# A graph network on one core: the counts of destinations are gathered from a table in DRAM

## What is computed

```python
def _sage_conv(x, src, dst, Wp, bp, Wl, bl, Wr):
    h = relu(x @ Wp.T + bp)
    agg = segment_sum(h[src], dst, num_segments=N)
    cnt = segment_sum(ones(src.shape[0]), dst, num_segments=N)
    agg = agg / maximum(cnt, 1.0)[:, None]
    return agg @ Wl.T + bl + x @ Wr.T
```

## Time and profile before

| | |
|---|---|
| median of 3 runs | 1517.86 us (1517.79 to 1518.0) |
| profiled execution | 1517.14 us, of which the span from first to last instruction is 1515.0 us |
| TensorE busy | 1492.6 us, 99% |
| VectorE busy | 981.2 us, 65% |
| ScalarE busy | 687.1 us, 45% |
| GpSimd busy | 578.6 us, 38% |
| DMA engines | 193 GB/s in the mean |

### The profile page before, as it was taken

The page is one execution under the profiler, slowest core; times in us unless marked ns, Lnnn a source line. Parts: engine busy times, 40 slices in busy tenths (PEclk is TensorE's granted clock), DMA queues, the critical chain, the costliest instruction groups (busy, mean ns, idle before and its releaser), DMA issues.

```text
span 1515.0 us, 21400 instructions
## 1 busy us (share of the span) xinstructions
PE 1492.6 (99%) x7295; PEld 1221.5 (81%) x7295; DVE 981.2 (65%) x2164; ACT 687.1 (45%) x1267; POOL 578.6 (38%) x534
## 2 busy tenths in 40 slices
PE   7999999999999999999999999999999999999997
PEld 5787887888888888888888888888888888888886
DVE  7999975655555687777565655557766666555552
ACT  5545452232233577767322323357676652322322
POOL 4737754344323100100434442323354366444323
PEclk9999999999999999999999999999999999999999
DMA  8897877555554878887645555489999986455434
GB/s 301 319 377 249 271 249 238 111 90 89 93 85 56 242 263 306 271 275 253 216 108 90 88 93 88 54 244 320 345 329 324 328 292 207 80 89 90 73 45 60
DMA packets 152855, 291.72 MB, mean 193 GB/s; under 512 B 19885, under 2 KB 19948, under 8 KB 152620
## 3 DMA queue, kind: packets, MB, share of 16 engines
q1 hardware_dynamic: 123708, 224.81, 43.3%
q0 software_dynamic: 28464, 64.51, 24.7%
q10 hardware_dynamic: 576, 1.05, 0.2%
HBM read 132.33 MB, written 157.92 MB: 192 GB/s over the span
## 4 chain that ended last, share of the span: by engine, by line
PE 89%; DMA 4%; DVE 3%; issue 2%; POOL 1%; ACT 1%; SPq 0%; POOLq 0%; ACTq 0%; DVEq 0%
PE bank L737 12%; PE bank L736 12%; PE bank L738 12%; PE bank L724 9%; PE bank L820 7%; PE bank L822 7%; PE bank L821 7%; PE bank L841 7%; PE bank L843 7%; PE bank L842 7%; DMA node_x<-xn 2%; DVE stats L1073 1%; DVE rows_out L1103 1%; DVE h_low L1047 1%; DMA rows_in<-node_x,sorted_src 1%
## 5 line engine op out<-in xcount | busy, mean ns | idle before, releaser
L736 PE MATMUL bank<-w_high,h_low 128*128 128x512 f32 x900 | 374.6, 416 | 0.0
L737 PE MATMUL bank<-w_low,h_high 128*128 128x512 f32 x900 | 356.3, 396 | 0.0
L738 PE MATMUL bank<-w_high,h_high 128*128 128x512 f32 x900 | 354.5, 394 | 0.0
L981 ACT ACTIVATE h_high<-h_pre 128x500 fp32r<-128x500 f32 x120 | 74.6, 622 | 449.0 <-DVE h_pre L1284 449.0
L594 POOL DMA_INDIRECT rows_in<-node_x,sorted_src x120 | 124.1, 1034 | 274.6 <-PE bank L724 199.8
L927 ACT ACTIVATE h_high<-bank 128x512 fp32r<-128x512 f32 x221 | 131.4, 595 | 155.2 <-PE bank L724 155.0
L738 PEld LDWEIGHTS bank<-w_high,h_high 128*128 128x128 f32 x900 | 169.3, 188 | 40.3
L1050 DVE TENSOR_TENSOR h_low<-bank,h_high 128x512 fp32r<-128x512 f32 x152 | 105.0, 692 | 146.4 <-ACT h_high L927 144.5
L961 ACT ACTIVATE xn<-rows_in,off,rstd 128x512 f32<-128x512 f32 x237 | 189.4, 806 | 13.6 <-issue 9.0
L820 PE MATMUL bank<-xt_low,w_high 128*128 128x500 f32 x480 | 194.5, 405 | 0.0
L736 PEld LDWEIGHTS bank<-w_high,h_low 128*128 128x128 f32 x900 | 169.8, 189 | 30.3
(11 more groups left out here) (127 smaller groups left out, 2209.1 us busy)
## 6 DMA issues: line engine op xcount, KB each, us to landing
node_x<-xn SPq DMA_DIRECT2D x237, 256.0 KB, 3.9
rows_in<-node_z SPq DMA_DIRECT2D x158, 256.0 KB, 4.4
node_z<-rows_out SPq DMA_DIRECT2D x142, 256.0 KB, 2.8
out<-rows_out SPq DMA_DIRECT2D x79, 256.0 KB, 3.5
rows_in<-x SPq DMA_DIRECT2D x78, 256.0 KB, 4.6
residual<-x SPq DMA_DIRECT2D x78, 256.0 KB, 4.3
node_z<-bias_z SPq DMA_DIRECT2D x16, 256.0 KB, 3.6
rows_in<-node_x SPq DMA_DIRECT2D x16, 256.0 KB, 2.6
```

The costliest lines, as they stand in the source:

```text
L736: nc.tensor.matmul(psum, low[:, k, :], w_high("r", l)[:, k, :], start=(k == 0), stop=False)
L737: nc.tensor.matmul(psum, high[:, k, :], w_low("r", l)[:, k, :], start=False, stop=False)
L738: last = nc.tensor.matmul(psum, high[:, k, :], w_high("r", l)[:, k, :], start=False, stop=(k == K - 1))
```

## The change

The counts no longer travel with the edges. The table of 128 x 128 counts is stored to DRAM as it is (by SP, one step after DVE's copy). When the edges are in order, GpSimd gathers the count of each edge's destination from this table, with an indirect DMA of 125 single numbers for each edge tile, 40 in all. They stand in GpSimd's program behind the load of `carry` and ahead of the row gathers. DVE takes the reciprocal in the first layer's edge phase, after the first step of it. The differences, their splitting, the masks, the look-up products and the reads of them go, and the stores of edges no longer wait for them. The work on the sorted edges is moved from step 61 to step 54.

```diff
-STEP_LOOKUP = 27
-LOOKUPS = 2
-STEP_SORTED = 61
+STEP_SORTED = 54
...
+        count_table = nc.dram_tensor("count_table", [P * P, 1], F32).ap()
...
+                    if l == 0 and i == STEP_COUNTED + 1:
+                        sp.wait_ge(counts_copied, 1)
+                        sp.dma_start(count_table.rearrange("(p c) a -> p (c a)", c=P), counts
+                                     ).then_inc(counts_stored, DMA)
...
-            def reach_mask(t):
...
             def store_edges(t):
 
                 pool.wait_ge(rows_placed, t // SPREAD + 1)
-                pool.wait_ge(count_read, t + 1)
...
+            def gather_counts(t):
+
+                G.indirect_dma_start(
+                    out=count_of[0:EDGE_ROWS, t:t + 1], out_offset=None, in_=count_table,
+                    in_offset=bass.IndirectOffsetOnAxis(ap=count_row[0:EDGE_ROWS, t:t + 1], axis=0)
+                ).then_inc(counts_gathered, DMA)
...
             for t in range(EDGE_TILES):
                 count_masks(t)
-            stored = 0
             for t in range(EDGE_TILES):
-                reach_mask(t)
-                if t % LOOKUPS == LOOKUPS - 1 and t >= 2 * LOOKUPS:
-                    store_edges(stored)
-                    stored += 1
-            for t in range(stored, EDGE_TILES):
                 store_edges(t)
...
+            pool.wait_ge(count_rows, 1)
+            pool.wait_ge(counts_stored, DMA)
+            for t in range(EDGE_TILES):
+                gather_counts(t)
...
-            def steps_of_counts():
...
-            def lookup(t):
...
-            def make_steps():
...
-            def count_digits():
...
-                V.reciprocal(share[0:EDGE_ROWS, :], in_order[0:EDGE_ROWS, :, 2]).then_inc(share_done, 1)
+                V.tensor_scalar(count_row[0:EDGE_ROWS, :], number[0:EDGE_ROWS, :], -1.0, None, ALU.add
+                                ).then_inc(count_rows, 1)
...
-            def read_count(t):
...
+            def shares():
+                dve.wait_ge(counts_gathered, DMA * EDGE_TILES)
+                V.reciprocal(share[0:EDGE_ROWS, :], count_of[0:EDGE_ROWS, :]).then_inc(share_done, 1)
...
+                    if l == 0 and s == 0:
+                        shares()
```

More of the change, by code:

```diff
@@ L15 @@
 DMA = 16
-CONSTS = 6
+CONSTS = 5
 IN_RING = 8
@@ L24 @@
 HOT_RING = 4
-STEP_RING = 4
 ROW_CHUNKS = 5
@@ L182, in sage_kernel @@
         edge_columns = residual[0:GROUPS, 1, 0:GROUP_ROWS]
-        counts, count_steps, steps_lo_f, steps_i0, steps_i1, steps_b = spare[0:6]
-        steps_i = [steps_i0.bitcast(I32), steps_i1.bitcast(I32)]
-        steps_b = steps_b.bitcast(BF16).rearrange("p (a c) -> p a c", a=2)
+        counts = spare[0]
         xt_high = [sb(f"xt_high{i}", [P, K * GROUP_ROWS], F32R) for i in range(2)]
@@ L223, in sage_kernel @@
         counts_copied = sem("counts_copied")
[L224 to L229, removed]
+        counts_stored = sem("counts_stored")
+        count_rows = sem("count_rows")
+        counts_gathered = sem("counts_gathered")
         share_done = sem("share_done")
@@ L766, in count @@
                                  start=(t == 0), stop=(t == EDGE_TILES - 1)).then_inc(counted, 1)
-            def steps_of_counts():
[L769 to L772, removed]
             def turn_carry():
                 pe.wait_ge(continues_done, 1)
-                pe.wait_ge(count_read, EDGE_TILES)
+                pe.wait_ge(counts_copied, 1)
                 nc.tensor.transpose(bank[2][0:EDGE_TILES, 0:EDGE_ROWS], continues[0:EDGE_ROWS, :],
                                     ident[0:EDGE_ROWS, 0:EDGE_ROWS]).then_inc(carry_turned, 1)
-            def lookup(t):
[L781 to L791, removed]
             def shift_p(l):
@@ L859, in _ @@
                             count((i - STEP_COUNT) * COUNTS + q)
-                    if l == 0 and i == STEP_COUNTED + 1:
-                        steps_of_counts()
                     if l == 0 and i == STEP_SORTED + 1:
                         turn_carry()
-                    if l == 0 and STEP_LOOKUP <= i < STEP_LOOKUP + EDGE_TILES // LOOKUPS:
-                        for q in range(LOOKUPS):
-                            lookup((i - STEP_LOOKUP) * LOOKUPS + q)
                     if l and i == STEP_SHIFT_P:
@@ L1214, in copy_carry @@
                 V.tensor_copy(carry_row[0:EDGE_TILES, :], bank[2][0:EDGE_TILES, 0:EDGE_ROWS]).then_inc(carry_copied, 1)
-            def read_count(t):
-                step, q = t // LOOKUPS, t % LOOKUPS
-                dve.wait_ge(looked_up, (step + 1) * LOOKUPS)
-                if step:
-                    dve.wait_ge(count_read, step * LOOKUPS)
-                V.scalar_tensor_tensor(out=unread[0:EDGE_ROWS, q, :], in0=column_no[0:EDGE_ROWS, 0:P],
-                                       scalar=lo_f[0:EDGE_ROWS, t:t + 1],
-                                       in1=bank[2 + step % 2][0:EDGE_ROWS, q * P:(q + 1) * P],
-                                       op0=ALU.is_equal, op1=ALU.mult, accum_out=edges[0:EDGE_ROWS, t, 2:3]
-                                       ).then_inc(count_read, 1)
+            def shares():
+                dve.wait_ge(counts_gathered, DMA * EDGE_TILES)
+                V.reciprocal(share[0:EDGE_ROWS, :], count_of[0:EDGE_ROWS, :]).then_inc(share_done, 1)
             def shift_part(l, m, k):
@@ L1326, in _ @@
                         copy_counts()
-                    if l == 0 and i == STEP_COUNTED + 2:
-                        count_digits()
                     if l == 0 and i == STEP_SORTED:
@@ L1332, in _ @@
                         copy_carry()
-                    if l == 0 and STEP_LOOKUP <= i - 1 < STEP_LOOKUP + EDGE_TILES // LOOKUPS:
-                        for q in range(LOOKUPS):
-                            read_count((i - 1 - STEP_LOOKUP) * LOOKUPS + q)
                     if 0 <= i - STEP_SPLIT_P < K:
```

32 lines of the change are left out of this document (2 added, 30 removed).

## The result

The changed kernel takes 1549.71 us in the median (1547.95 to 1551.35), the kernel before in the same rounds 1517.93 us. The ratio is 1.021, with an interval of 1.020 to 1.022. The forecast was 1537.9 us with a range up to 1547 us. So the sign was right, and the size was out of the range by 2.7 us: +31.8 us where +20.0 us stood.

A forecast was written before the change was run, and what follows sets the result against it. TensorE, busy 99%, bounds the kernel, but GpSimd's first row gathers decide when the edge phase starts. Row gathers 18.0 us later plus 2.0 us restart give +20.0 us: 1517.9 to 1537.9 us, range 1529 to 1547 us.

The forecast's parts named there:

- What goes: TensorE, node steps 27 to 46: look-up matmuls and the steps-of-counts product go, 6.8 us together; DVE and GpSimd savings costed at nothing.
- What moves: Sorted edges' work on DVE from 224.50 to 195.1 us, carries' store to 201.6, GpSimd free at 205.6.
- The restart: TensorE after its long wait at the first edge tile: slow transposes and first product, costing 2.0 us.
- The place: First layer's edge phase starts when GpSimd's first row gathers land, not when TensorE is free; one wait of 14 to 27 us.
- The rivals 3 and 4: 3: sorted edges late at DVE's step 54, 1541 us, chance 0.08; 4: low pitch, no slow restart, 1530 us, chance 0.15.
- Forty of them are 56 us: GpSimd, ahead of the row gathers: forty count gathers at 1.40 us pitch start the first row gather 18.0 us later.
- rival 2: GpSimd's queue fills and stalls 3.3 us among the count gathers, at the high pitch: +26.9 us, 1545 us; chance 0.15.
- I see nothing later that takes it back: TensorE from 249 us on has next to no idle time, so the delay stays to the end.
- Rival 1: Count gathers on GpSimd hidden before the row gathers, only savings stay: 1511 us at best; chance 0.05 faster, 0.02 within 0.2%.

## Why the forecast was too low

**Right.** *What goes*: TensorE's last node product starts at 240.08, as "at about 240 us" had it, and the steps 27 to 46 take 3.23 to 3.24 us each (the 3.42 us that the prediction names for a step of before is read a little low, transposes to transposes none takes under 3.44; nothing hangs on it). *What moves*: the order loads are issued at 185.96 (forecast 186) and DVE starts on the sorted edges, without a wait, at

```profile
195.21 0.18 DVE L1134 CAST sorted_src<-in_order 128x40 int32<-128x40 f32 x1
```

(forecast 195.1); the carries' store is at 202.23 (201.6). The stall ahead of the last store came again, 5.28 us this time, and fitted, because the stores as a whole ran early. *The restart*: 2.04 us, of a forecast of 2.0, and the two runs with products in the wait show that it is the idle time's. That the size is met so well is in part luck: the forecast was 1.7 us for the product and 0.4 us for the transposes, and it was 2.04 us for the product, while the slow transposes (0.76 instead of 0.41 us) were hidden, since the second tile followed the first more closely than before. *The place*: one wait, at the first edge tile, made by GpSimd's order. The Trainium skill says in "TensorE: Matmul & The Clock Gate", Part 1 (The HAM clock gate), that an idle array drops to 1.2 GHz; the trace agrees here, with a granted clock of 0.50 beside the 4.91 us. The 1.00 of the earlier trace rows beside a product as slow is no measurement: the trace of the kernel before has its first entry of the clock at 14.5 us, and there its matmuls go from 0.63 us (the one at 13.96) to 0.39 us (14.68). *The rivals 3 and 4* did not come: the sorted edges were in time, and the restart was slow.

**The step that failed: "Forty of them are 56 us ... The first row gather then starts at 205.6 + 56 = 261.6 us".** It started at 269.97, 8.4 us later. Three terms of it were off:
- The pitch is (268.47 + 1.50 - 207.43 - 2.19) / 40 = 1.51 us, not 1.40: 4.4 us. I stood between two rows and took a value between them. The issue takes as long as that of the stores in the earlier trace rows, 1,202 ns against 1,189 ns, though direction and size differ; the trait that the two share is the 125 rows. The run with 128 rows shows that it was this trait: 955 ns, in the same direction and with as many bytes for each row. So of these three it is the number of rows and neither the direction nor the bytes that made the difference, and I weighed three traits alike. No number but 125 and 128 was tried.
- The stall of rival 2 came, once: 268.47 - 264.78 = 3.69 us where the pitch is 1.50, 2.2 us. It stands ahead of the fortieth transfer: in the stores of edges in all 16 traces, among them the kernel before, where the first twenty stores stood among masks and not in a row; and in the counts in all five traces with forty 125-row gathers ahead of the row gathers. It didn't come with twenty gathers, with forty of 128 rows or with forty spread among the row gathers. "It has been seen once, under a loaded DMA" was my reason for 0.15, and it was a poor one: what had been seen once in one try came every time. That a queue fills, as rival 2 supposes, no run shows.
- GpSimd was free at 207.43, not at 205.6, 1.8 us: the store of the carries 0.6 us later, and its landing 3.75 us of wait instead of the 2.5 of before. This wait is not a fixed amount: 1.84 to 4.54 us in the experiments.

So the times of rival 2 in its single form are what came about up to the first edge tiles: it had +26.9 us, and 26.3 + 2.0 = 28.3 were measured there. The 1.4 us between are made of a longer pitch and a later start against a shorter stall.

**The step that was missing: "I see nothing later that takes it back"** looked only for time that would be made up. The same instructions ran slower, by 4.5 us in all, since the change of buffers moved the operands. Without these 4.5 us the time would have been 1545.2 us, inside the range; with them the range's upper bound of 1547 us was passed. The two failures make up the miss: 8.3 us of delay and 4.5 us of pace are 12.8 us of span, and the medians are 11.8 us above the forecast. I had counted the removed and the added instructions, but not the removed and the added buffers.

**Rival 1** (hidden gathers) was rightly held for unlikely, at this place: at 1.26 us, the shortest pitch that was seen, forty gathers from 207.9 still end at 258. But its reckoning was a hint. It asked how many gathers fit ahead of the row gathers (26 us of room were measured, some 17 gathers), and the others could have been put behind them; the better order would have been in the forecast.

## What to carry to other kernels

A gather costs its issuing engine about the same whatever it moves: here a pitch of 1.26 us for 128 rows, be it 512 bytes or 256 KB, and 1.51 us for 125 rows. So cost a change that trades work of a busy engine for many such transfers by their number, from the row with the same count of rows, and look first at what stands behind them in GpSimd's program; put those behind that nobody waits for soon. When a kernel with a saturated engine gains or loses buffers, compare the distance of the same instruction at the beginning and at the end: a drift without waits was the addresses here, and an experiment should hold them fixed. When runs come from several chips, look in the traces for gaps that belong to the chip before comparing two kernels across them.

## What the runs showed of the hardware that was not expected

- The issue of an indirect gather of 128 rows takes 0.95 us with 4 bytes or 2 KB a row, that of a transfer of 125 rows 1.20 us (4 bytes a row, gathered) or 1.19 us (16 bytes, stored), each with a gap of 0.30 us, where they stand in a row. The 125 rows take longer than the 128; no other number was tried.
- Ahead of the fortieth indirect DMA of 125 rows of a kind GpSimd stalls: 3.6 to 5.4 us of idle time in the stores of edges in all 16 traces, 2.5 us in the count gathers in five of five. Forty gathers of 128 rows, twenty of 125 and forty of 125 among the row gathers show none.
- After 4.31 us of standing TensorE restarted at the lower clock; after waits of 0.75 and 1.19 us it didn't.
- The place of the buffers in SBUF changes the pace of otherwise equal matmuls by less than a nanosecond each, 4.3 to 5.0 us of this kernel. A shift by 60 bytes alone gave 1.1 us; the property is open.
- On the chips on which the kernel before took 1526 to 1527 us, TensorE stood 4.0 to 5.8 us in sum with no cause in the profile in four kernels, and 32 and 34 us where forty 128-row gathers of single numbers ran in a row. In ten traces from the other chips there was no such gap.
